# Small vector steps of a first attention layer moved from VectorE to ScalarE and GpSimd, in a three-layer attention program

## The chip, the cores and the metric

The program runs on one core of one Trainium2 chip, as one launch. The metric is the device time of that core in microseconds. Before the change the median of three runs is 1432.54 us (1431.04 to 1433.38).

## What is computed

Sixteen sequences of 256 tokens by 128 channels pass through a gated depthwise convolution, an attention whose softmax is taken apart in chunks of 64 keys, a layer norm, and then two layers of windowed attention with a gated MLP. The change touches only the first part. Cut to what matters, in float32:

```python
context = x.mean(axis=1)
gate = sigmoid(context @ w_kgen.T + b_kgen).mean(axis=1)        # one number a sequence, of 3 sigmoids
y = (depthwise_conv3(x) + b_conv) * gate                        # 3 taps over the tokens
q, k, v = y @ w_q.T, y @ w_k.T, y @ w_v.T                       # 16 query heads, 4 key heads, 64 wide
w = softmax(q @ k.T / 8) inside each chunk c of 64 keys         # 4 chunks
sum_w = w.sum(-1)                                               # the share of each chunk
out = sum_c(sum_w[c] * (w[c] @ v[c])) / (sum_c(sum_w[c]) + 1e-9)
x = layernorm(x + out @ w_o.T)
```

The kernel applies one factor to the exponentials of each head and chunk: with s their sum, the share is s * (1/s), the total adds the four shares and 1e-9, and the factor is (1/s) * share / total.

## The kernel before

Every engine has its own instruction stream, written out by hand, and streams meet only at semaphores. The first attention ("stage A") goes through the sequences two to a turn, in 8 turns. A sequence has two tiles of 128 queries, and a tile has four steps, g = 0 to 3, one for each key head with its four query heads. So a sequence takes 8 steps, and each engine's `a_body` walks through the same steps. At step s:

- TensorE (PE) transposes the scaled exponentials of step s-7 (L1291, into `wT`'s banks), computes the scores of step s (L1304), at some steps fills a bank for the sequence after this one (transposes of x, gate logits, at tile 1 the projections q, k and v from `hT`: L1264, L1266, L1268), multiplies the transposed weights of step s-7 by v (L1330), and at g = 3 does the output projection (L1341). The scores of step s need the subtraction of step s-2, since two pairs of banks hold them.
- VectorE (DVE) takes the maxima `mx` of the scores (L1030) and subtracts them (L1036, into `probs`), and adds up the exponentials of step s-2 (L1004, `sums`). At g = 1 this sum stands ahead of the step's maxima and is the last of a tile, so the factors `coef` follow at once (L989 to L996, seven short instructions, each waiting for the one before). The convolution `conv` of the next sequence stands at tile 0, g = 2 (L947 to L953), its gate and `hT` at tile 1, g = 0 (L959 to L967), the residual sum `y` and its statistics `mv` at g = 3 (L1053 to L1059), the end of the layer norm `xo` at g = 2 (L1065).
- ScalarE (ACT) copies `wT` out of its banks (L783), then projections (L757, L762, L767), then takes the exponentials of step s-1 (L796) and copies `oT` (L802).
- GpSimd (POOL) multiplies `probs` of step s-5 by `coef` (L625), so that a tile's four products begin at g = 1, and computes the layer norm's 1/sqrt (L636, L639) at g = 0. In the first turn it also splits the layers' weights into two parts (L613, L615), in steps 0 to 5, after a wait for all weights and four table products (L607).
- SyncE (SP) issues the DMAs; none of its code changes.

After the last turn a "drain" finishes the late steps and already begins with the layers that follow.

## Time and profile before

| what | us |
|---|---|
| median of three runs | 1432.54 |
| the profiled execution, its own time | 1430.35 |
| its span on the core | 1428.5 |
| stage A, up to the last maxima and subtractions | about 655 |
| the layers behind it | the rest, about 770 |

The profile shows each instruction with its start and duration, from one execution. In rows that group instructions ("lines"), the columns are: line, engine, operation, output<-inputs, shapes, count, then busy us and mean ns of one, then the idle us of the engine just before them and who ended it. A timeline row has start us, duration us, engine, line, operation, names, shapes, count, and in brackets the idle time before it. The duration of a run of instructions (x2) is from its first start to its last end. On PE each matrix product of float32 shows as two records. Neighbours overlap by some 0.08 us: differences of starts add up exactly, durations do not.

### The profile page before, as it was taken

The numbers are of one execution on the slowest core, as the hardware profiler recorded it, in microseconds if no ns is written. First come the engines' busy times: TensorE is split into PE (matmuls) and PEld (weight loads), VectorE is DVE, ScalarE is ACT, GpSimd is POOL, SyncE is SP. The second block draws the span as 40 slices with busy tenths as digits, with TensorE's granted clock in tenths as the row PEclk, the third lists the DMA queues.
The fourth block names the chain that finished last, engine by engine and source line by source line (L and its number), as shares of the span: only waits on it lengthen the run. The fifth ranks groups of instructions, "written<-read, shape, count | busy, mean of one in ns | idle before, by whom it ended". The sixth has DMA issues, their size and how long they took to land.

```text
span 1428.5 us, 36014 instructions
## 1 busy us (share of the span) xinstructions
PE 1258.4 (88%) x12288; PEld 984.8 (69%) x12288; DVE 1262.2 (88%) x2418; ACT 943.0 (66%) x1708; POOL 905.3 (63%) x787
## 2 busy tenths in 40 slices
PE   5889989998889898997789889898988999999985
PEld 3667767777667676775567777677776777777764
DVE  4999999999999999997688888888888899988974
ACT  3566666566666566564478777777877778787772
POOL 0733443344433443346798888888888899999972
PEclk8899999999999999999899999999999999999999
DMA  5000000000000000000111111121111211212111
GB/s 167 1 10 13 12 5 10 11 11 11 9 11 11 11 2 11 8 8 12 36 43 45 41 41 40 39 49 35 44 41 45 55 45 46 49 42 55 43 32 33
DMA packets 87051, 44.14 MB, mean 31 GB/s; under 512 B 43908, under 2 KB 80176, under 8 KB 86960
## 3 DMA queue, kind: packets, MB, share of 16 engines
q1 hardware_dynamic: 86960, 42.95, 12.0%
q8 instruction: 54, 0.88, 0.3%
q14 instruction: 37, 0.30, 0.1%
HBM read 19.86 MB, written 6.29 MB: 18 GB/s over the span
## 4 chain that ended last, share of the span: by engine, by line
DVE 45%; issue 19%; POOL 17%; PE 16%; DVEq 1%; ACT 1%; POOLq 0%; DMA 0%; SPq 0%; ACTq 0%
DVE sums L1004 9%; DVE probs L1036 7%; POOL rnorm L660 7%; DVE mx L1030 5%; POOL kT L668 4%; PE bank L1389 3%; POOL kT L649 3%; DVE xo L1065 2%; DVE hc L1102 2%; DVE qT L1084 2%; PE bank L1376 2%; PE bank L1473 2%; PE bank L1445 2%; DVE f_sum L1184 2%; DVE conv L947 1%
## 5 line engine op out<-in xcount | busy, mean ns | idle before, releaser
L625 POOL TENSOR_TENSOR probs<-probs,coef 128x1024 f32<-128x1024 f32 x128 | 239.5, 1901 | 201.0 <-DVE coef L996 201.0
L796 ACT ACTIVATE probs<-probs 128x1024 f32<-128x1024 f32 x128 | 134.8, 1053 | 98.8 <-DVE probs L1036 98.2
L649 POOL TENSOR_TENSOR kT<-qT 128x512 f32<-128x512 f32 x128 | 162.7, 1272 | 53.8 <-DVE qT L1084 53.6
L660 POOL TENSOR_TENSOR rnorm<-norm,halves 128x16 f32<-128x16 f32 x64 | 188.9, 2952 | 6.1 <-POOL norm L657 1.5
L1291 PE MATMUL bank<-ident,probs 128*128 128x128 f32 x1024 | 144.0, 286 | 49.2 <-POOL probs L625 49.2
L783 ACT ACTIVATE wT<-bank 128x512 f32<-128x512 f32 x256 | 138.6, 596 | 63.8 <-PE bank L1291 62.8
L1030 DVE TENSOR_REDUCE mx<-bank 128x8 f32<-128x512 f32 x256 | 164.0, 682 | 14.3 <-PE bank L1304 12.9
L1036 DVE TENSOR_TENSOR probs<-bank,mx 128x512 f32<-128x512 f32 x256 | 163.7, 682 | 0.0
L1291 PEld LDWEIGHTS bank<-ident,probs 128*128 128x128 f32 x1024 | 116.2, 145 | 68.3 <-POOL probs L625 57.4
L1304 PE MATMUL bank<-kT,qT 64*128 64x256 f32 x1024 | 157.2, 429 | 5.4 <-DVE probs L1036 5.4
L1004 DVE TENSOR_REDUCE sums<-probs 128x16 f32<-128x1024 f32 x128 | 153.4, 1211 | 0.0
L1330 PE MATMUL bank<-wT,v 128*64 128x128 f32 x2048 | 145.5, 286 | 8.6 <-DVE gate L942 4.7
L1202 DVE TENSOR_REDUCE fmx<-bank 128x4 f32<-128x512 f32 x128 | 82.5, 686 | 77.9 <-PE bank L1445 77.9
L1330 PEld LDWEIGHTS bank<-wT,v 128*64 128x64 f32 x2048 | 114.2, 141 | 47.3 <-issue 24.7
L668 POOL TENSOR_TENSOR kT<-kT,rnorm 128x512 f32<-128x512 f32 x128 | 131.1, 1045 | 4.3 <-POOL rnorm L660 0.7
L1304 PEld LDWEIGHTS bank<-kT,qT 64*128 64x128 f32 x1024 | 94.9, 200 | 37.1 <-issue 23.6
L1389 PE MATMUL bank<-hT,w 128*128 128x256 f32 (+1 forms) x384 | 97.5, 390 | 25.0 <-DVE mid L1167 23.2
L1376 PE MATMUL bank<-ident,kT 128*128 128x128 f32 x512 | 82.6, 285 | 38.6 <-POOL kT L668 37.3
L636 POOL TENSOR_TENSOR rstd<-mv,eps 128x1 f32<-128x1 f32 x32 | 6.2, 192 | 156.5 <-DVE mv L1059 156.5
L1376 PEld LDWEIGHTS bank<-ident,kT 128*128 128x128 f32 x512 | 57.0, 142 | 69.9 <-POOL kT L668 37.2
L721 POOL TENSOR_TENSOR probs<-probs,f_rsum 128x640 f32<-128x640 f32 x64 | 80.4, 1256 | 37.4 <-DVE f_rsum L1188 37.4
L1371 PE MATMUL bank<-wqkv_high,fhT_high 128*128 128x512 f32 x192 | 93.8, 489 | 3.9 <-DVE fhT_low L1152 1.0
(120 smaller groups left out, 3097.8 us busy)
## 6 DMA issues: line engine op xcount, KB each, us to landing
probs<-f_v SPq DMA_DIRECT2D x96, 128.0 KB, 2.3
res<-stage_x SPq DMA_DIRECT2D x48, 128.0 KB, 3.8
xn<-in_x SPq DMA_DIRECT2D x16, 128.0 KB, 2.2
xr<-in_x SPq DMA_DIRECT2D x16, 128.0 KB, 2.1
stage_x<-xo SPq DMA_DIRECT2D x32, 64.0 KB, 1.6
hn<-stage_x SPq DMA_DIRECT2D x32, 64.0 KB
mn<-mid SPq DMA_DIRECT2D x64, 32.0 KB
stage_x<-yo SPq DMA_DIRECT2D x16, 128.0 KB, 2.1
```

What stands on the lines that cost most here:

```text
L625: nc.gpsimd.tensor_tensor(out=e[:, :, :, :], in0=e[:, :, :, :], in1=coef[r][:, 2, A_REP * ng:A_REP * (ng + 1), :].unsqueeze(3).broadcast_t ...
L649: nc.gpsimd.tensor_tensor(out=qk[m][:, :, :], in0=on_self[m % 2][:, :, :], in1=on_partner[m % 2][:, :, :], op=ALU.add).then_inc(added, 1)
L660: nc.gpsimd.tensor_tensor(out=rnorm[:, at], in0=norm2[:, 1, at], in1=halves[:, 0:2 * F_HEADS], op=ALU.pow).then_inc(rnorm_set, 1)
L668: nc.gpsimd.tensor_tensor(out=qk[m][:, :, :], in0=qk[m][:, :, :], in1=rnorm[:, F_HEADS * m:F_HEADS * (m + 1)].unsqueeze(2).broadcast_to([P ...
L1004: nc.vector.tensor_reduce(sums[at % 2][:, A_REP * gg:A_REP * (gg + 1), :], E[(s - SUM_LAG) % E_RING][:, :, :, :], AX.X, ALU.add).then_inc( ...
L1030: ins = nc.vector.tensor_reduce(m[:, 2 * k:2 * k + 2, :], both[k][:, :].rearrange("p (h c k) -> p h c k", h=2, c=CHUNKS), AX.X, ALU.max)
L1036: ins = nc.vector.tensor_tensor(e[:, 2 * k:2 * k + 2, :, :], both[k][:, :].rearrange("p (h c k) -> p h c k", h=2, c=CHUNKS), m[:, 2 * k:2 ...
L1291: ins = nc.tensor.transpose(banks[4 + hp][:, P * (2 * kb + hh):P * (2 * kb + hh + 1)], e[:, 2 * hh + hp, 2 * kb:2 * kb + 2, :], ident[:, :])
L1304: ins = nc.tensor.matmul(banks[2 * (s % 2) + h % 2][:, SEQ * (h // 2):SEQ * (h // 2 + 1)], qT[p][lo:lo + A_HD, 2 * g + h // 2, P * tile:P ...
L1330: ins = nc.tensor.matmul(bank[A_HD * hh:A_HD * (hh + 1), P * hp:P * (hp + 1)], v[ap][:, kb, A_HD * og:A_HD * (og + 1)], wT[hp][:, kb, hh, ...
L1376: ins = nc.tensor.transpose(bank[:, P * block_of:P * (block_of + 1)], flat[:, P * block_of:P * (block_of + 1)], ident[:, :])
L1389: return nc.tensor.matmul(bank[0:rows, col:col + SEQ], w1[layer][:, at:at + rows], hT2[par][:, :], start=True, stop=True)
```

## The change

On VectorE only the two reciprocals of the factors, the reciprocal and the sum of the gate, and `y` with its statistics stay. The rest moves:

- The three taps of the convolution become three scaled copies on ScalarE (`taps`, tile 0, g = 1), added up by GpSimd (`convolution`, ahead of the product at tile 0, g = 2). The product with the gate (`gated_input`) and the end of the layer norm (`xo`) become scaled copies at the end of ScalarE's steps at tile 1, g = 0 and at g = 2. For `xo` GpSimd prepares a shift, the mean times -1 times 1/sqrt.
- GpSimd makes the shares, their total and the factors, ahead of a tile's first product (`shares`, `factors`), and the gate's denominators (`gate_denominator`, with the 1/3 of the mean in it).
- On VectorE the second reciprocal of the factors (`total_inverted`) stands between the maxima and the subtraction of g = 1, and the gate (`gated`) moves from ahead of the maxima at tile 1, g = 0 to behind the subtraction.
- On GpSimd the wait for the weights and the table products stand behind the first sequence's gate and convolution.

The diff, without the lines that define tiles, semaphores and constants, and without the bodies of the VectorE functions that go (they stand in the kernel above):

```diff
             pool.wait_ge(consts_set, N_CONSTS)
...
+            def shares(j, r):
+                c, tt, k = coef[r], total[r], SHARE_STEPS * j
+                pool.wait_ge(inverse_set, j + 1)
+                nc.gpsimd.tensor_tensor(out=c[:, 1, :, :], in0=sums[r][:, :, :], in1=c[:, 0, :, :], op=ALU.mult).then_inc(share_step, 1)
+                pool.wait_ge(share_step, k + 1)
+                nc.gpsimd.tensor_tensor(out=c[:, 2, :, 0:2], in0=c[:, 1, :, 0:2], in1=c[:, 1, :, 2:4], op=ALU.add).then_inc(share_step, 1)
+                pool.wait_ge(share_step, k + 2)
+                nc.gpsimd.tensor_tensor(out=tt[:, 0, :], in0=c[:, 2, :, 0], in1=c[:, 2, :, 1], op=ALU.add).then_inc(share_step, 1)
+                pool.wait_ge(share_step, k + 3)
+                nc.gpsimd.tensor_tensor(out=tt[:, 1, :], in0=tt[:, 0, :], in1=tiny[:, :], op=ALU.add).then_inc(share_step, 1)
+            def factors(j, r):
+                c, tt = coef[r], total[r]
+                pool.wait_ge(total_set, j + 1)
+                nc.gpsimd.tensor_tensor(out=c[:, 1, :, :], in0=c[:, 1, :, :],
+                                        in1=tt[:, 2, :].unsqueeze(2).broadcast_to([P, A_HEADS, CHUNKS]), op=ALU.mult).then_inc(coef_set, 1)
+                pool.wait_ge(coef_set, 2 * j + 1)
+                nc.gpsimd.tensor_tensor(out=c[:, 2, :, :], in0=c[:, 0, :, :], in1=c[:, 1, :, :], op=ALU.mult).then_inc(coef_set, 1)
+            def gate_denominator(b):
+                pool.wait_ge(gate_exp, b + 1)
+                nc.gpsimd.tensor_tensor(out=gate[:, 2, :], in0=gate[:, 1, :], in1=one3[:, 0, :], op=ALU.add).then_inc(gate_plus, 1)
+                pool.wait_ge(gate_plus, 2 * b + 1)
+                nc.gpsimd.tensor_tensor(out=gate[:, 2, :], in0=gate[:, 2, :], in1=one3[:, 1, :], op=ALU.mult).then_inc(gate_plus, 1)
+            def convolution(b):
+                pool.wait_ge(taps_set, b + 1)
+                nc.gpsimd.tensor_tensor(out=conv[:, 1, :], in0=conv[:, 0, :], in1=conv[:, 1, :], op=ALU.add).then_inc(conv_set, 1)
+                pool.wait_ge(conv_set, 2 * b + 1)
+                nc.gpsimd.tensor_tensor(out=conv[:, 2, :], in0=conv[:, 1, :], in1=conv[:, 2, :], op=ALU.add).then_inc(conv_set, 1)
...
                 for s, slot, p, tile, g in steps(i, turn, beside):
+                    if tile == 0 and g == 2 and prepares(turn, p):
+                        convolution(PAIR * i + p + 1)
+                    if tile == 1 and g == 0 and prepares(turn, p):
+                        gate_denominator(PAIR * i + p + 1)
                     if exists(turn, s, NORM_LAG):
...
                         r = at % 2
-                        wait(pool, coef_step, COEF_STEPS * (A_SLOTS * i + at + 1))
+                        if ng == 0:
+                            shares(A_SLOTS * i + at, r)
+                            factors(A_SLOTS * i + at, r)
+                        wait(pool, coef_set, 2 * (A_SLOTS * i + at + 1))
                         e = E[(s - NORM_LAG) % E_RING]
...
-            stage_a(pool, a_body)
+                        nc.gpsimd.tensor_tensor(out=rstd[r][:, 2:3], in0=mv[r][:, 0:1], in1=minus[:, 0:1], op=ALU.mult).then_inc(shift_set, 1)
+                        pool.wait_ge(rstd_set, j + 1)
+                        pool.wait_ge(shift_set, 2 * j + 1)
+                        nc.gpsimd.tensor_tensor(out=rstd[r][:, 3:4], in0=rstd[r][:, 2:3], in1=rstd[r][:, 1:2], op=ALU.mult).then_inc(shift_set, 1)
+            def a_pre():
+                gate_denominator(0)
+                convolution(0)
+                pool.wait_ge(weights_in, 16 * N_WEIGHTS)
+                for l in range(LAYERS):
+                    for tile in range(TILES):
+                        nc.gpsimd.tensor_tensor(out=table[l][:, tile, :, :], in0=rotary[:, tile, :, :], in1=qk_scale[l][:, :, :],
+                                                op=ALU.mult).then_inc(tables_set, 1)
+            stage_a(pool, a_body, a_pre)
...
+            def taps(b):
+                act.wait_ge(read["xT"], b + 1)
+                nc.scalar.activation(conv[:, 0, :], xT[:, 1:SEQ + 1], ACT.Identity, bias=bconv[:, 0:1], scale=wconv[:, 1:2])
+                nc.scalar.activation(conv[:, 1, :], xT[:, 0:SEQ], ACT.Copy, scale=wconv[:, 0:1])
+                nc.scalar.activation(conv[:, 2, :], xT[:, 2:SEQ + 2], ACT.Copy, scale=wconv[:, 2:3]).then_inc(taps_set, 1)
+            def gated_input(b):
+                act.wait_ge(conv_set, 2 * b + 2)
+                act.wait_ge(gate_step, GATE_STEPS * (b + 1))
+                wait(act, made["v"], b)
+                nc.scalar.activation(hT[:, :], conv[:, 2, :], ACT.Copy, scale=gate_sum[:, 0:1]).then_inc(hT_set, 1)
...
                 act.wait_ge(consts_set, N_CONSTS)
+                act.wait_ge(gate_weights_in, 16 * N_GATE_WEIGHTS)
                 x_transposed(0, 0, "pre", 0)
+                taps(0)
                 gate_exponential(0)
+                gated_input(0)
                 for kind, local in A_BANKS.pre[2:]:
...
                             x_transposed(i, p + 1, turn, PAIR * i + p + 1)
+                        if g == 1:
+                            taps(PAIR * i + p + 1)
                         if g == 3:
...
                                              banks[6 + A_BANKS.bank("o", s - PV_LAG, "middle")][:, 0:2 * P], ACT.Copy).then_inc(read["o"], 1)
+                    if prepares(turn, p) and tile == 1 and g == 0:
+                        gated_input(PAIR * i + p + 1)
+                    if g == LN_LAG % A_KV and exists(turn, s, LN_LAG):
+                        at = (s - LN_LAG) // A_KV
+                        j, r = A_SLOTS * i + at, at % 2
+                        act.wait_ge(shift_set, 2 * j + 2)
+                        wait(act, xo_out[r], 16 * (2 * i + at // 2))
+                        nc.scalar.activation(xo[r][:, :], y[r][:, :], ACT.Identity, bias=rstd[r][:, 3:4], scale=rstd[r][:, 1:2]).then_inc(xo_set, 1)
...
-            def convolution(b):
...
-                dve.wait_ge(gate_exp, b + 1)
-                nc.vector.tensor_scalar_add(gate[:, 2, :], gate[:, 1, :], 1.0).then_inc(gate_step, 1)
+                dve.wait_ge(gate_plus, 2 * b + 2)
+                nc.vector.reciprocal(gate[:, 3, :], gate[:, 2, :]).then_inc(gate_step, 1)
                 dve.wait_ge(gate_step, GATE_STEPS * b + 1)
-                nc.vector.reciprocal(gate[:, 3, :], gate[:, 2, :]).then_inc(gate_step, 1)
-                dve.wait_ge(gate_step, GATE_STEPS * b + 2)
+                wait(dve, hT_set, b)
                 nc.vector.tensor_reduce(gate_sum[:, :], gate[:, 3, :], AX.X, ALU.add).then_inc(gate_step, 1)
-                dve.wait_ge(gate_step, GATE_STEPS * b + 3)
-                dve.wait_ge(conv_step, 3 * b + 3)
-                wait(dve, made["v"], b)
-                nc.vector.tensor_scalar(hT[:, :], conv[:, 2, :], gate_sum[:, 0:1], 1.0 / KS,
-                                        ALU.mult, ALU.mult).then_inc(hT_set, 1)
...
                 gate_logit(0, 0, "pre")
-                convolution(0)
                 gated(0)
...
-            def factors(j, r):
...
+            def inverted(j, r):
                 dve.wait_ge(sum_done, A_KV * (j + 1))
-                wait(dve, normed, A_KV * (j - 1))
-                link(nc.vector.reciprocal(c[:, 0, :, :], sums[r][:, :, :]), 1)
-                link(nc.vector.tensor_tensor(c[:, 1, :, :], sums[r][:, :, :], c[:, 0, :, :], ALU.mult), 2)
-                link(nc.vector.tensor_reduce(tt[:, 0, :], c[:, 1, :, :], AX.X, ALU.add), 3)
-                link(nc.vector.tensor_scalar_add(tt[:, 1, :], tt[:, 0, :], 1e-9), 4)
-                link(nc.vector.reciprocal(tt[:, 2, :], tt[:, 1, :]), 5)
-                link(nc.vector.tensor_tensor(c[:, 1, :, :], c[:, 1, :, :],
-                                             tt[:, 2, :].unsqueeze(2).broadcast_to([P, A_HEADS, CHUNKS]), ALU.mult), 6)
-                link(nc.vector.tensor_tensor(c[:, 2, :, :], c[:, 0, :, :], c[:, 1, :, :], ALU.mult), 7)
+                nc.vector.reciprocal(coef[r][:, 0, :, :], sums[r][:, :, :]).then_inc(inverse_set, 1)
+            def total_inverted(i, turn, s):
+                if exists(turn, s, SUM_LAG):
+                    at = (s - SUM_LAG) // A_KV
+                    j, r = A_SLOTS * i + at, at % 2
+                    dve.wait_ge(share_step, SHARE_STEPS * (j + 1))
+                    nc.vector.reciprocal(total[r][:, 2, :], total[r][:, 1, :]).then_inc(total_set, 1)
...
                     dve.wait_ge(exp_done, n + 1)
+                    if gg == 0:
+                        wait(dve, coef_set, 2 * (A_SLOTS * i + at - 1))
                     nc.vector.tensor_reduce(sums[at % 2][:, A_REP * gg:A_REP * (gg + 1), :], E[(s - SUM_LAG) % E_RING][:, :, :, :],
...
                     if gg == A_KV - 1:
-                        factors(A_SLOTS * i + at, at % 2)
+                        inverted(A_SLOTS * i + at, at % 2)
...
                         gate_weights(PAIR * i + p + 1)
-                    if tile == 1 and g == 0 and prepares(turn, p):
-                        gated(PAIR * i + p + 1)
                     if g == 1:
...
                             ins.then_inc(max_set, 1)
+                        if g == 1:
+                            total_inverted(i, turn, s)
                         wait(dve, wT_made, 2 * (n - E_RING) + 2)
...
                         ins.then_inc(sub_done, 1)
+                    elif g == 1:
+                        total_inverted(i, turn, s)
                     if tile == 0 and g == 2 and prepares(turn, p):
                         gate_logit(PAIR * i + p + 1, p + 1, turn)
+                    if tile == 1 and g == 0 and prepares(turn, p):
+                        gated(PAIR * i + p + 1)
                     if g != 1:
                         summed(i, turn, s)
-                    if prepares(turn, p):
-                        b = PAIR * i + p + 1
-                        if tile == 0 and g == 2:
-                            convolution(b)
                     if g == OUT_LAG % A_KV and exists(turn, s, OUT_LAG):
...
                         dve.wait_ge(made["out"], j + 1)
+                        wait(dve, xo_set, j - 1)
                         dve.wait_ge(xr_in[(at // TILES) % 2], 16 * (i + at // TILES // PAIR + 1))
...
                         nc.vector.bn_aggr(mv[r][:, :], stat[r][:, :]).then_inc(y_step, 1)
-                    if g == LN_LAG % A_KV and exists(turn, s, LN_LAG):
-                        at = (s - LN_LAG) // A_KV
-                        j, r = A_SLOTS * i + at, at % 2
-                        dve.wait_ge(rstd_set, j + 1)
-                        wait(dve, xo_out[r], 16 * (2 * i + at // 2))
-                        nc.vector.tensor_scalar(xo[r][:, :], y[r][:, :], mv[r][:, 0:1], rstd[r][:, 1:2],
-                                                ALU.subtract, ALU.mult).then_inc(xo_set, 1)
```

How the order of instructions changes, at three places. A row is a line of the program, an operation, and its names and output shape. First VectorE, from the gated input at tile 1, g = 0, to the maxima of g = 1. Before:

```order
L967 TENSOR_SCALAR hT<-conv,gate_sum 128x256
L1030 TENSOR_REDUCE mx<-bank 128x8 x2
L1036 TENSOR_TENSOR probs<-bank,mx 128x512 x2
L1004 TENSOR_REDUCE sums<-probs 128x16 x2
L989 RECIPROCAL coef<-sums 128x64
L990 TENSOR_TENSOR coef<-sums,coef 128x64
L991 TENSOR_REDUCE total<-coef 128x16
L992 TENSOR_SCALAR total<-total 128x16
L993 RECIPROCAL total<-total 128x16
L994 TENSOR_TENSOR coef<-coef,total 128x64
L996 TENSOR_TENSOR coef<-coef 128x64
L1030 TENSOR_REDUCE mx<-bank 128x8 x2
```

The same stretch after the change:

```order
L1087 TENSOR_REDUCE mx<-bank 128x8 x2
L1095 TENSOR_TENSOR probs<-bank,mx 128x512 x2
L1030 RECIPROCAL gate<-gate 128x3
L1033 TENSOR_REDUCE gate_sum<-gate 128x1
L1063 TENSOR_REDUCE sums<-probs 128x16 x2
L1045 RECIPROCAL coef<-sums 128x64
L1087 TENSOR_REDUCE mx<-bank 128x8 x2
L1053 RECIPROCAL total<-total 128x16
L1095 TENSOR_TENSOR probs<-bank,mx 128x512 x2
```

The five steps between the two sums and the maxima have become one, the second reciprocal has moved in behind the maxima, and the gate's two steps stand behind the subtraction.

GpSimd's stream in one sequence, from one tile's factors to the end of its products. After the change (before it, only the products, L625, stand here):

```order
L622 TENSOR_TENSOR coef<-sums,coef 128x64
L624 TENSOR_TENSOR coef<-coef 128x16x2
L626 TENSOR_TENSOR total<-coef 128x16
L628 TENSOR_TENSOR total<-total,tiny 128x16
L634 TENSOR_TENSOR coef<-coef,total 128x64
L637 TENSOR_TENSOR coef<-coef 128x64
L667 TENSOR_TENSOR probs<-probs,coef 128x1024
L649 TENSOR_TENSOR conv<-conv 128x256
L651 TENSOR_TENSOR conv<-conv 128x256
L667 TENSOR_TENSOR probs<-probs,coef 128x1024 x2
L642 TENSOR_TENSOR gate<-gate,one 128x3
L644 TENSOR_TENSOR gate<-gate,one 128x3
```

Six small instructions now stand ahead of a tile's first product, two of the convolution between the first and the second, and two of the gate between the third and the fourth.

GpSimd in the first turn, at the weights' splits. Before:

```order
L613 CAST wqkv_high<-wqkv 128x512
L615 TENSOR_TENSOR wqkv_low<-wqkv,wqkv_high 128x512
L613 CAST wqkv_high<-wqkv 128x512
L615 TENSOR_TENSOR wqkv_low<-wqkv,wqkv_high 128x512
L625 TENSOR_TENSOR probs<-probs,coef 128x1024
L613 CAST wqkv_high<-wqkv 128x512
L615 TENSOR_TENSOR wqkv_low<-wqkv,wqkv_high 128x512
L625 TENSOR_TENSOR probs<-probs,coef 128x1024 x7
```

After, from the end of the second split (of six) to the first factors:

```order
L615 TENSOR_TENSOR wqkv_low<-wqkv,wqkv_high 128x512
L649 TENSOR_TENSOR conv<-conv 128x256
L651 TENSOR_TENSOR conv<-conv 128x256
L613 CAST wqkv_high<-wqkv 128x512
L615 TENSOR_TENSOR wqkv_low<-wqkv,wqkv_high 128x512
L613 CAST wqkv_high<-wqkv 128x512
L615 TENSOR_TENSOR wqkv_low<-wqkv,wqkv_high 128x512
L642 TENSOR_TENSOR gate<-gate,one 128x3
L644 TENSOR_TENSOR gate<-gate,one 128x3
L613 CAST wqkv_high<-wqkv 128x512
L615 TENSOR_TENSOR wqkv_low<-wqkv,wqkv_high 128x512
L622 TENSOR_TENSOR coef<-sums,coef 128x64
```

The second sequence's convolution stands behind two splits and its gate behind four.

## Rows read from the trace of the kernel before

**Rows 1.** The profile's page, its first part.

```profile
PE 1258.4 (88%) x12288; PEld 984.8 (69%) x12288; DVE 1262.2 (88%) x2418; ACT 943.0 (66%) x1708; POOL 905.3 (63%) x787
```

**Rows 2.** Busy us (instructions) of PE, PEld, DVE, ACT, POOL; then granted clock.

```profile
148.50:590.60 442.10, 397.62 (x3474) 311.62 (x3474) 428.26 (x782) 271.93 (x485) 180.65 (x133) 0.97 0.03 10
```

**Rows 3.** PE, groups by line, from 148.5 to 590.6 us.

```profile
L1291 PE MATMUL bank<-ident,probs 128*128 128x128 f32 x704 | 98.3, 284 | 29.9 <-POOL probs L625 29.9
L1264 PE MATMUL bank<-hT,wq 128*128 128x256 f32 x176 | 46.5, 397 | 9.8 <-DVE hT L967 9.8
...
L1247 PE MATMUL bank<-ident,xn 128*128 128x128 f32 x22 | 4.8, 300 | 0.0
L1254 PE MATMUL bank<-wk_ctx,ones 128*128 128x3 f32 x22 | 4.2, 263 | 0.0
```

**Rows 4.** VectorE, timeline of one tile's last sum, factors and next maxima.

```profile
301.19 1.21 DVE L1004 TENSOR_REDUCE sums<-probs 128x16 f32<-128x1024 f32 x1
302.43 0.55 DVE L989 RECIPROCAL coef<-sums 128x64 f32<-128x64 f32 x1
...
304.43 1.28 DVE L1030 TENSOR_REDUCE mx<-bank 128x8 f32<-128x512 f32 x2
305.63 1.28 DVE L1036 TENSOR_TENSOR probs<-bank,mx 128x512 f32<-128x512 f32 x2
```

**Rows 5.** VectorE, groups by line, from 148.5 to 590.6 us.

```profile
L1065 DVE TENSOR_SCALAR xo<-y,mv,rstd 128x128 f32<-128x128 f32 x22 | 23.8, 1081 | 0.0
L947 DVE TENSOR_SCALAR conv<-xT,wconv,bconv 128x256 f32<-128x256 f32 x11 | 20.0, 1815 | 0.0
...
L993 DVE RECIPROCAL total<-total 128x16 f32<-128x16 f32 x22 | 5.6, 253 | 0.8
L953 DVE SCALAR_TENSOR_TENSOR conv<-xT,wconv,conv 128x256 f32<-128x256 f32 x11 | 5.3, 485 | 0.4
...
L994 DVE TENSOR_TENSOR coef<-coef,total 128x64 f32<-128x64 f32 x22 | 5.0, 225 | 0.8
```

**Rows 6.** PE, timeline: a wait and what follows it; then two steps without waits.

```profile
306.55 1.09 PE L1291 MATMUL bank<-ident,probs 128*128 128x128 f32 x8 [1.85 <-POOL probs L625]
307.57 2.03 PE L1304 MATMUL bank<-kT,qT 64*128 64x256 f32 x8
...
617.44 1.13 PE L1304 MATMUL bank<-kT,qT 64*128 64x256 f32 x8
...
620.55 1.13 PE L1304 MATMUL bank<-kT,qT 64*128 64x256 f32 x8
```

**Rows 7.** GpSimd, groups by line: two from 148.5 us on, two from 640 us on.

```profile
L625 POOL TENSOR_TENSOR probs<-probs,coef 128x1024 f32<-128x1024 f32 x89 | 166.5, 1901 | 144.3 <-DVE coef L996 144.3
...
L636 POOL TENSOR_TENSOR rstd<-mv,eps 128x1 f32<-128x1 f32 x22 | 4.2, 190 | 115.1 <-DVE mv L1059 115.1
...
L649 POOL TENSOR_TENSOR kT<-qT 128x512 f32<-128x512 f32 x128 | 162.7, 1272 | 53.8 <-DVE qT L1084 53.6
...
L657 POOL TENSOR_SCALAR norm<-norm 128x16 f32<-128x16 f32 x64 | 16.1, 252 | 0.1
```

**Rows 8.** ScalarE, groups by line, from 148.5 to 590.6 us.

```profile
L802 ACT ACTIVATE oT<-bank 128x256 f32<-128x256 f32 x88 | 33.0, 375 | 7.1 <-PE bank L1330 6.4
```

**Rows 9.** Timelines of the first turn: GpSimd's tables; VectorE's gate; its maxima of step 8.

```profile
33.64 2.78 POOL L607 TENSOR_TENSOR table<-rotary,qk_scale 128x256 f32<-128x256 f32 x4 [31.72 <-DMA qk_scale<-in_k_scale]
...
36.35 0.16 DVE L959 TENSOR_SCALAR gate<-gate 128x3 f32<-128x3 f32 x1
...
57.01 1.29 DVE L1030 TENSOR_REDUCE mx<-bank 128x8 f32<-128x512 f32 x2 [1.42 <-PE bank L1304]
```

**Rows 10.** VectorE, timeline: two maxima one tile apart in the last sequence; the drain's end.

```profile
625.62 1.28 DVE L1030 TENSOR_REDUCE mx<-bank 128x8 f32<-128x512 f32 x2
...
644.38 1.28 DVE L1030 TENSOR_REDUCE mx<-bank 128x8 f32<-128x512 f32 x2
...
687.23 3.48 DVE L1065 TENSOR_SCALAR xo<-y,mv,rstd 128x128 f32<-128x128 f32 x1 [0.92 <-POOL rstd L639]
```

41 lines of the change are left out of this document (14 added, 27 removed).

## The prediction

> **What bounds the kernel now.** I read the page first, for the engines' shares: PE and VectorE both stand at 88% of the span [rows 1], which decides nothing, since stage A and the layers have different limits. So I cut out a stretch of the steady state: from 148.50 to 590.60 us the gate logits of eleven sequences pass, so a sequence takes 442.1 / 11 = 40.19 us. In it VectorE is busy for 428.26 us, 97%, PE for 397.62 (36.15 a sequence), GpSimd for 180.65 and ScalarE for 271.93 [rows 2]. The groups of PE then show that its idle time of 44.5 us is waiting for others: 29.9 for GpSimd's first product of a tile, which itself waits for `coef` from VectorE, and 9.8 for `hT`, also from VectorE [rows 3]. VectorE's own groups show next to no waits [rows 5]. VectorE sets the pace of stage A, and PE is 4 us a sequence behind it as the next limit.
>
> **What leaves VectorE.** In the eleven sequences `xo` costs 23.8 us and the first step of the convolution 20.0, the two others 5.3 each with 0.4 of dependency idle [rows 5]. The five factor steps that go are between 3.8 and 5.0 busy us each, 23.4 together, with about 4 us of idle between them (0.8 each, as in the row of L994). `hT` and the gate's first step make 5.4, with 0.9 idle. The sum is 43.8 + 10.6 + 0.8 + 27.4 + 6.3 = 89 us, or 8.1 us a sequence. That leaves 40.2 - 8.1 = 32.1 us of VectorE a sequence. Most of `xo` and of the convolution is no arithmetic: 1081 and 1815 ns on the mean, as they stand beside GpSimd's products. If only VectorE counted, 14 sequences would give back 113 us. But PE needs 36.15 us a sequence as its busy time stands, so I take PE as the next limit, and ask what it will wait for.
>
> **What PE will wait for at a tile's first product.** The chain from the scores of g = 0 to PE's transposes at g = 3 is now split over three engines. VectorE: maxima and subtraction 1.2 each (304.43 to 305.63 for one), sum of g = 0 1.12, with the 0.13 of `wk_ctx`, the last sum 1.24 (301.19 to 302.43), reciprocal 0.55: 5.44 us [rows 4]. Then GpSimd. For its small steps the trace has 190 ns for one element a partition, 252 for 16 (one input) and 1272 for 512 [rows 7]; a line through the first and the last gives 0.19 + 0.0021 a element, so 0.3 for 64, 0.25 for 32, 0.2 for 16. With 0.07 to 0.08 from one step to the next that depends on it, as between L989 and L990, the four steps of the shares are 0.07 + 0.30 + 0.08 + 0.25 + 0.08 + 0.2 + 0.08 + 0.2 = 1.3 us. Beside them VectorE does the maxima of g = 1, 1.2 us, so it waits 0.1 and this reciprocal, 0.25, comes at 1.35. Two more steps of 64, 0.75 with their gaps, and the product, 1.9 [rows 7], end 4.3 us after the first reciprocal. The whole is 0.1 + 5.44 + 4.3 = 9.85 us after the scores. PE in that time does the rest of step 0, steps 1 and 2: three steps of 3.11 (617.44 to 620.55), less the transposes and scores of step 0, 1.02 and 1.07 [rows 6], plus 0.44 for x and 0.38 for the gate logits [rows 3]: 8.1 us. So at tile 0 PE waits about 1.8 us. At tile 1 four fills of about 1 us (46.5 us for 44 of them [rows 3]) stand in place of the 0.8: 11.1 against 9.85 + 0.4 for the gate: no wait, 0.9 of slack. Bounds of the six small GpSimd steps, of 1.5 us in all: 190 ns each from below would take 0.3 off; VectorE's 225 ns for 64 [rows 5] times GpSimd's 1.27 to VectorE's 0.64 at 512 (half of 1.28, rows 4) gives 0.42 each, or about 1 us more with the short rows of four elements; I take the line, as it passes through this engine's own rows.
>
> The Trainium skill ("GPSIMD Engine Reference", section 4.1) puts elementwise work on VectorE and calls GpSimd about 2x slower for two inputs, which speaks against these six steps. By it 64 elements would be 0.45 us instead of 0.3, the tile's wait some 0.7 us longer and the whole change worth 10 us less. The row of 190 ns for one element says that the fixed part is no larger than VectorE's, so I don't take it for the small ones.
>
> **The gated input.** `hT` was ahead of the maxima of tile 1, g = 0; now the gate stands behind the subtraction, and ScalarE makes `hT` at the end of its step. From the scores: 0.1 + 2.4 + 0.4 + 0.07 + 0.35 + 0.1 = 3.4 us, against 3.1 of PE (products of step 4, transposes and scores of step 5). PE waits 0.3. ScalarE is held there until 0.35 us before, and its copies `wT` of the next step come late, but end before PE has done its two fills, 1.9 us.
>
> **What costs nothing.** ScalarE gains three taps, `hT` and two `xo` a sequence, at most 375 ns each like `oT` [rows 8], 2.2 us on 24.7; the exponentials that the taps push back by 0.9 are wanted by VectorE a step later. GpSimd gains 2 x 1.5 for the factors, 2 x 0.7 for the convolution, 0.5 for the gate and 2 x 0.4 for the shift, on 16.4: it is busy 22 of 38 us. The convolution's steps delay the second product by 1.4 us, PE wants that 5 us after the first. If ScalarE's cover went, each late `wT` would cost PE its length, 0.6 us.
>
> **The slow clock.** After the wait of 1.85 us PE's scores take 2.03 us instead of 1.13 [rows 6]; the granted clock of the stretch is 0.97 of 2.4 GHz [rows 2]. PE's 36.15 a sequence holds that share; with waits of the same length once a sequence I leave it in.
>
> **The sum.** A sequence takes 36.15 + 1.8 + 0.3 = 38.2 us, 2.0 less than now. That holds for the 14 sequences from step 8 to the last that prepares another: -28 us.
>
> First turn: GpSimd is free for work only when the weights are there, 33.64, and the tables done, 36.4 [rows 9]. Then come two splits of 1.95, the second sequence's convolution 1.4, two splits, and the gate 0.5: 46.1. VectorE wanted the gate at 36.35 and now stands until 46.1, ahead of two sums and the first reciprocal, which ends at 49.4. Shares to first product: 53.6, where it was 48.1. PE then has the transposes, scores, two fills, products and the next transposes and scores, 7.2 us: the maxima of step 8 come at about 61, where they were at 57.01 [rows 9]. +4 us, between +2 (if the splits overlap what VectorE had lost there anyway) and +7.
>
> Last sequence: no fills, so PE's step stretch is 7.25 and the wait 2.6; a tile is 14.3 (four steps of 3.11, and 1.9 for the output projection's sixteen records at the pace of eight transposes in 1.02) + 2.6 + about 1.5 for slow clock = 18.4 against 18.76 [rows 10]: -0.6 for two, between -4 and +2. Drain: `xo` on VectorE stands 3.48 us behind GpSimd's clears, and the first scores of the layers wait for what is behind it [rows 10]; on ScalarE it is short, -2; GpSimd's longer chain gives back 1: -1. The layers don't change.
>
> 1430.35 + 4 - 28 - 0.6 - 1 = 1404.8 for an execution like the profiled one, which lies 2.2 us under the median of 1432.54. On the median: 1407, and I say 1406.
>
> **Rivals.**
> - *The handover is hidden, and PE runs without waits.* For it: VectorE would have 4 us of slack a sequence, and the wait of tile 0 is a difference of two sums of 8 and 10 us. Against: it would take 1.8 us less on a chain whose long parts are rows. 36.15 a sequence: 14 x -4.0 + 2.4 = 1377 to 1383, say 1380. 15%.
> - *GpSimd's small steps take 0.4 to 0.5 us, or the slow clock comes with each wait.* One us more at tile 0 (tile 1 keeps its slack), or 0.9 more of slow products a sequence: 14 us back, 1420. For it: the wait of 1.85 did bring the slow clock; against: in this stretch only about every second did. 20%.
> - *Slower: GpSimd's handover becomes the limit.* Place: the six steps ahead of a tile's first product. Each us added costs 1 us at tile 0 and, beyond 0.9, 1 us at tile 1; with 2.0 us of gain a sequence the change loses from 1.5 us added on, that is from 0.5 us a small step. At 0.75 us each, 3 us added, a sequence takes 38.2 + 3 + 2.1 = 43.3, and the program 1432 + 14 x 3.1 + 2 = 1478. For it: the steps read rows of 2 or 4 elements or one in four, which no row of GpSimd here shows. Against: 252 ns for 16 elements. 10%.
> - *VectorE's two new waits* (shares ahead of the subtraction, the gate's denominators) *eat the slack*, so that stage A keeps its pace: 1430 to 1435. It needs 6 us a sequence of waiting. 5%.
>
> **How the numbers follow.** The forecast has 50%; its own range, from the bounds above (0.3 less and 1 more on the chain of tile 0, +2 to +7 in the first turn, -4 to +2 at the end), is 1396 to 1419. With the two neighbours the range that should hold 8 in 10 is 1384 to 1427. About 0.2%, 3 us, is what a measurement of this kernel can tell from no change. Faster by more than that: 50 + 15 + 18 = 83%; within it 5% (the last rival and the upper edge of the second); slower 12%.
>
> **What would show it.** In a stretch of eleven sequences: 38.2 us each; VectorE near 85% busy, PE near 95%; PE's waits for GpSimd at tile 0 near 1.8 us and none at tile 1; its wait for `hT` at 0.3; GpSimd's six steps 0.2 to 0.3 us each; VectorE's wait ahead of the second reciprocal 0.1. In the first turn a stand of VectorE from 37 to 46 us. It would be wrong if small GpSimd steps are above 0.5 us, if `wT` waits on ScalarE appear in PE's list in microseconds, or if PE's busy time moves by more than 0.9 us a sequence from 36.15.

## The result, and the profile after

| what | median us (runs) | ratio to before, 95% interval |
|---|---|---|
| before, beside it | 1432.21 (4) | |
| after | 1419.45 (1417.34 to 1420.7, 4) | 0.9909 (0.9892 to 0.9927) |

The change makes the program 12.8 us faster. The forecast was 1406, 26 us faster: the sign was right, and a little less than half of the gain came. 1419.45 lies just outside the forecast's own range (1396 to 1419), inside the wide one. One run of the kernel of experiment 10 below, of 2333 us, was disturbed and is in no interval.

The first part of the page of the kernel after answers to [rows 1], and the windows answer to [rows 2]. The first window holds eleven sequences, from one gate logit to another, the second the rest of stage A, up to the layers' first scores.

```profile
PE 1252.5 (88%) x12288; PEld 978.7 (69%) x12288; DVE 1146.5 (81%) x2146; ACT 976.5 (69%) x1804; POOL 996.2 (70%) x1111
```

```profile
153.19:583.77 430.58, 396.04 (x3479) 308.78 (x3477) 352.08 (x595) 293.66 (x550) 243.18 (x352) 0.98 0.04 10
...
583.80:685.30 101.50, 86.28 (x765) 68.23 (x763) 65.91 (x112) 55.34 (x101) 66.27 (x86) 0.92 0.04 11
```

A sequence now takes 430.58 / 11 = 39.14 us, where it took 40.19. VectorE went from 97% to 352.08 / 430.58 = 82% busy (85% were forecast), so it left the path as forecast. PE is busy 36.00 us a sequence, also as forecast (36.15), but that is 92% of the sequence and not the 95% of the forecast. The other 3.14 us are waits, and the groups of PE, which answer to [rows 3], name them:

```profile
L1382 PE MATMUL bank<-wT,v 128*64 128x128 f32 x1408 | 100.4, 287 | 8.6 <-ACT qT L826 8.6
L1343 PE MATMUL bank<-ident,probs 128*128 128x128 f32 x707 | 95.4, 278 | 21.7 <-POOL probs L667 21.7
L1316 PE MATMUL bank<-hT,wq 128*128 128x256 f32 x176 | 46.5, 397 | 4.2 <-ACT hT L814 4.2
```

21.7 / 11 = 1.97 us is the wait for the first product at tile 0 (none at tile 1), 0.38 the wait for `hT`, and 0.78 is a wait for ScalarE that the forecast did not have. 36.00 + 1.97 + 0.78 + 0.38 = 39.13.

The handover, in the timelines of VectorE, GpSimd and PE after (start us, us, engine, ...), beside [rows 4, 6]:

```profile
304.46 0.55 DVE L1045 RECIPROCAL coef<-sums 128x64 f32<-128x64 f32 x1
...
306.36 0.25 DVE L1053 RECIPROCAL total<-total 128x16 f32<-128x16 f32 x1 [0.21 <-POOL total L628]
...
305.09 0.32 POOL L622 TENSOR_TENSOR coef<-sums,coef 128x64 f32<-128x64 f32 x1 [5.13 <-DVE coef L1045]
305.49 0.24 POOL L624 TENSOR_TENSOR coef<-coef 128x32 f32<-128x32 f32 x1
305.81 0.22 POOL L626 TENSOR_TENSOR total<-coef 128x16 f32<-128x16 f32 x1
306.11 0.22 POOL L628 TENSOR_TENSOR total<-total,tiny 128x16 f32<-128x16 f32 x1
306.69 0.30 POOL L634 TENSOR_TENSOR coef<-coef,total 128x64 f32<-128x64 f32 x1 [0.37 <-DVE total L1053]
307.07 0.32 POOL L637 TENSOR_TENSOR coef<-coef 128x64 f32<-128x64 f32 x1
307.46 1.90 POOL L667 TENSOR_TENSOR probs<-probs,coef 128x1024 f32<-128x1024 f32 x1
...
309.42 1.09 PE L1343 MATMUL bank<-ident,probs 128*128 128x128 f32 x8 [1.98 <-POOL probs L667]
```

The six small steps take 0.22 to 0.32 us. From the reciprocal's end to the product's, 305.0 to 309.36, are 4.35 us; 4.3 were forecast.

Where the time went, in the two profiled executions: VectorE reads the third gate logit at 73.25 instead of 68.69 us (+4.6). From it to the sixteenth are 510.5 instead of 521.9 us (-11.4, thirteen sequences). From there to the layers' first scores are 101.6 instead of 103.4 (-1.8), and the layers are 1.0 shorter: -9.6 in the span (1428.5 to 1418.9). The profiled execution of before was its fastest and that of after its slowest, so this sum is 3 us short of the difference of the medians.

### The profile page after: what moved, and what is told of

Read it like the earlier page. It is cut to its first block, busy times and chain, and to the rows that moved or that the text cites. A ratio compares the mean times of both kernels' runs of the same rounds, so it can differ in the third digit from the quotient of the medians.

```text
span 1418.9 us, 36244 instructions
## 1 busy us (share of the span) xinstructions
PE 1252.5 (88%) x12288; PEld 978.7 (69%) x12288; DVE 1146.5 (81%) x2146; ACT 976.5 (69%) x1804; POOL 996.2 (70%) x1111
## 4 chain that ended last, share of the span: by engine, by line
POOL 33%; issue 25%; PE 21%; DVE 16%; ACT 2%; SPq 2%; POOLq 1%; DVEq 0%; DMA 0%; ACTq 0%
POOL probs L667 9%; POOL rnorm L715 7%; POOL kT L723 4%; PE bank L1441 3%; POOL kT L704 3%; DVE hc L1154 2%; PE bank L1428 2%; PE bank L1525 2%; PE bank L1356 2%; PE bank L1497 2%; DVE qT L1136 2%; DVE f_sum L1236 2%; PE bank L1343 2%; PE bank L1393 2%; POOL probs L776 1%
## 5 line engine op out<-in xcount | busy, mean ns | idle before, releaser
L1343 PE MATMUL bank<-ident,probs 128*128 128x128 f32 x1024 | 139.9, 280 | 37.3 <-POOL probs L667 37.3
L1382 PE MATMUL bank<-wT,v 128*64 128x128 f32 x2048 | 147.5, 289 | 13.7 <-ACT qT L826 11.4
L1343 PEld LDWEIGHTS bank<-ident,probs 128*128 128x128 f32 x1024 | 112.9, 142 | 55.4 <-POOL probs L667 42.0
L622 POOL TENSOR_TENSOR coef<-sums,coef 128x64 f32<-128x64 f32 x32 | 10.3, 321 | 151.7 <-DVE coef L1045 151.7
```

The lines of the kernel that those rows point to most:

```text
L1343: ins = nc.tensor.transpose(banks[4 + hp][:, P * (2 * kb + hh):P * (2 * kb + hh + 1)], e[:, 2 * hh + hp, 2 * kb:2 * kb + 2, :], ident[:, :])
L1382: ins = nc.tensor.matmul(bank[A_HD * hh:A_HD * (hh + 1), P * hp:P * (hp + 1)], v[ap][:, kb, A_HD * og:A_HD * (og + 1)], wT[hp][:, kb, hh, ...
```

## Experiments

Each stands as its median of 4 to 7 runs and its ratio to runs of the kernel before on the same chip. Differences in us, where nothing else is said, are of medians. The kernel before had 1430.96 us beside experiments 1 to 4 and 1431.70 to 1431.90 beside the others, against 1432.21 beside after, so such a difference to after can be 1 us off.

**1. Only `xo` moved.** The kernel before, with `xo` on ScalarE at g = 2 and its shift on GpSimd:

```diff
+ nc.gpsimd.tensor_tensor(out=rstd[r][:, 2:3], in0=mv[r][:, 0:1], in1=minus[:, 0:1], op=ALU.mult)        # and the shift, on GpSimd
...
+ nc.scalar.activation(xo[r][:, :], y[r][:, :], ACT.Identity, bias=rstd[r][:, 3:4], scale=rstd[r][:, 1:2])  # behind oT at g = 2
...
- nc.vector.tensor_scalar(xo[r][:, :], y[r][:, :], mv[r][:, 0:1], rstd[r][:, 1:2], ALU.subtract, ALU.mult)
```

> The kernel before with one part of the change alone: the end of the layer norm (xo) on ScalarE, with GpSimd's shift; convolution, gate, factors stay on VectorE. Theory (PE's waits are the limit behind VectorE, and little has to leave VectorE to reach it): VectorE loses 23.8 us in 11 sequences, 2.2 of 40.2 us a sequence, and PE's 36.0 plus its waits fit under the 38.0 left. About 38.0 to 38.5 us a sequence, 14 x 1.7 to 2.2 us = 24 to 30 us less than before: 1403 to 1408, faster than the whole change (1419). Rival (each part gives a share of the whole gain as its share of the 8.1 us taken off VectorE): 2.2/8.1 of 13 us, 1429.

Measured: 1410.31 us, 0.9857 (0.9842 to 0.9872), a little above the 1403 to 1408 of the theory. One of the moves alone gives 21 us (against 1430.96 beside it), more than all of them. A sequence takes 430.26 / 11 = 39.11 us here, where the theory had 38.0 to 38.5, and the granted clock is 1.00 where it was 0.98 after. Window and groups of PE in the same eleven sequences:

```profile
147.26:577.52 430.26, 388.66 (x3476) 304.29 (x3476) 407.01 (x761) 276.21 (x507) 188.33 (x177) 1.00 0.03 10
```

```profile
L1337 PE MATMUL bank<-wT,v 128*64 128x128 f32 x1408 | 96.3, 279 | 10.0 <-DVE gate L955 8.6 <-ACT qT L764 0.9
L1298 PE MATMUL bank<-ident,probs 128*128 128x128 f32 x704 | 94.9, 278 | 20.2 <-POOL probs L628 20.2
L1271 PE MATMUL bank<-hT,wq 128*128 128x256 f32 x176 | 46.5, 397 | 11.3 <-DVE hT L980 11.3
```

VectorE is 95% busy and already has 10.8 us of waits for scores, so 2 us off it are enough: it and PE now bound each other, and what else is taken off VectorE can only shorten PE's waits.

The whole change does shorten them, from 430.26 - 388.66 = 41.6 us here to 430.58 - 396.04 = 34.5 us in the eleven sequences. But PE is busy 396.04 us instead of 388.66. Here the waits for products are two a sequence, of 0.6 to 0.7 and 1.1 to 1.2 us, with no slow clock behind them; after, one of 1.97 us stands in their place, often with the slow clock behind it (experiment 4 shows the rows). The two kernels' thirteen sequences differ by only 2.3 us (508.2 against 510.5). The rest of this kernel's lead lies outside them: its third gate logit comes 4.0 us earlier, as it leaves the first turn almost as it was, and from the last gate logit to the layers it takes 95.5 us instead of 101.6, with a granted clock of 0.98 instead of 0.92.

**2. The factors back on VectorE**, all else as after: `shares` and `factors` go from GpSimd, the seven-step function comes back behind the last sum.

```diff
...
- nc.vector.reciprocal(coef[r][:, 0, :, :], sums[r][:, :, :]).then_inc(inverse_set, 1)
...
+ factors(j, r)        # the seven steps L989 to L996 of before
```

> The changed kernel with one part undone: all seven factor steps on VectorE ahead of the maxima again; convolution, gate, xo stay moved. Theory (the handover to GpSimd and back sets PE's wait at tile 0): from the first reciprocal to GpSimd's first product 2.16 us instead of 3.0, PE's wait at tile 0 falls from 1.98 to about 1.1 us, VectorE has 34.4 us of work a sequence and still waits for PE. 14 x 0.85 = 12 us less than the changed kernel: about 1407. Rival (VectorE's load is what counts, any work given back to it costs): 1.15 us later maxima twice a sequence, +14 to +32 us: 1433 to 1450.

Measured: 1410.45 us, 0.9863 (0.9848 to 0.9879): 9 us better than after (7 by the ratios). PE's wait for the first product falls from 1.97 to 12.9 / 11 = 1.17 us, and its busy time from 36.00 to 388.77 / 11 = 35.34, with the clock at 1.00.

```profile
L1359 PE MATMUL bank<-wT,v 128*64 128x128 f32 x1408 | 96.3, 279 | 17.2 <-DVE gate L1000 8.6 <-ACT qT L802 8.6
L1320 PE MATMUL bank<-ident,probs 128*128 128x128 f32 x704 | 94.9, 278 | 12.9 <-POOL probs L643 12.9
```

The shorter chain is not the whole reason, though. VectorE now reads the gate logits late, and PE waits 8.6 / 11 = 0.78 us for their bank, which it did not after; the wait for `hT` grows from 0.38 to 0.63 us. All of PE's waits together went up, from 3.14 to 3.36 us a sequence. What fell is the time that it is busy: without one long wait, no group ran at the slow clock. So in this order of the kernel the split of the factor chain over two engines costs more than it gives, and the cost shows in the clock.

**3. TensorE's output projection ahead of the products at g = 3.** A test of my first reading of the 0.78 us, that PE waits there for `wT`. The table that gives the fills of banks 6 and 7 their order changes with it.

```diff
+ if g == OUT_LAG % A_KV and exists(turn, s, OUT_LAG):   # the output projection, moved up
      if late:                                            # the products of wT and v
```

> The changed kernel, with PE's output projection at g = 3 ahead of the products with v instead of behind them. Theory (PE's new wait of 0.79 us at tile 1, g = 3 is for wT copies that ScalarE makes late, behind kT, the exponentials, oT and xo, once a sequence): the 1.9 us of output projection cover it, 14 x 0.79 = 11 us less than the changed kernel: about 1408. Rival (ScalarE as a whole is behind, and the wait turns up at the next place that needs it): within 3 us of 1419.

Measured: 1426.19 us, 0.9967 (0.9956 to 0.9978). The theory falls, and 7 us more than after is outside the rival's 3 us too. The wait moved whole to the projection:

```profile
L1376 PE MATMUL bank<-wo,oT 128*128 128x128 f32 x352 | 49.3, 297 | 8.6 <-ACT qT L826 8.6
```

So it belongs to whatever comes first after the last fills at g = 3. The two banks 6 and 7 alternate, and the next user of the bank of the last q waits until ScalarE has read that q. ScalarE's timeline after, with the PE row that waits, shows why it reads late:

```profile
291.07 1.06 ACT L870 ACTIVATE probs<-probs 128x1024 f32<-128x1024 f32 x1
292.15 0.38 ACT L876 ACTIVATE oT<-bank 128x256 f32<-128x256 f32 x1
292.43 0.48 ACT L885 ACTIVATE xo<-y,rstd 128x128 f32<-128x128 f32 x1
292.81 1.07 ACT L855 ACTIVATE wT<-bank 128x512 f32<-128x512 f32 x2
293.77 0.60 ACT L826 ACTIVATE qT<-bank 128x512 f32<-128x512 f32 x1
...
294.50 1.09 PE L1382 MATMUL bank<-wT,v 128*64 128x128 f32 x16 [0.79 <-ACT qT L826]
```

PE filled the bank by 292.7; ScalarE comes to it at 293.77, behind the exponentials, `oT`, the new `xo` and two `wT`, on which PE would not have waited. Why this kernel is slower than after I followed only in part: eight of its thirteen sequences are slow ones, of 40.2 to 40.4 us, where after has seven of 39.9 to 40.0 (see the next experiment), and the others are 0.1 to 0.3 us longer too.

**4. The scores too ahead of the transposes at g = 3.** The transposes of g = 3 wait for the first product; the scores don't.

```diff
# on top of the edit of experiment 3; the two parts of the step stand in functions
- for part in (transposes, scores_of):
+ for part in ((scores_of, transposes) if g == OUT_LAG % A_KV else (transposes, scores_of)):
```

> As the run with the output projection first, and at g = 3 PE also does its scores ahead of its transposes. Theory (the wait of 1.98 us at tile 0 is the chain over VectorE and GpSimd, and PE has 1.07 us of scores that do not depend on it): the wait falls to 0.6 to 1.0 us, and with it the slow clock after it may go, 0 to 0.75 us a sequence. 14 x 1.0 to 1.7 us beyond the last run: 1385 to 1394. Rival (the scores of g = 3 wait themselves for the subtraction of g = 1, which is part of the same chain): no gain beyond the last run, 1408.

Measured: 1395.05 us, 0.9751 (0.9738 to 0.9765), 24 us under after and 31 under experiment 3, at the edge of the 1385 to 1394 of the theory. The wait of 1.97 became two short ones, as PE's timeline at tile 0 shows:

```profile
296.90 1.14 PE L1359 MATMUL bank<-kT,qT 64*128 64x256 f32 x8 [0.37 <-DVE probs L1095]
298.51 1.09 PE L1344 MATMUL bank<-ident,probs 128*128 128x128 f32 x8 [0.47 <-POOL probs L667]
```

The sequences show the rest of the gain. Between gate logits after there are two lengths, 38.4 to 38.5 and 39.9 to 40.0 us, seven of the thirteen long. In experiment 4 all thirteen lie between 37.55 and 37.76. A long one of after has the slow clock behind its wait:

```profile
190.94 1.09 PE L1343 MATMUL bank<-ident,probs 128*128 128x128 f32 x8 [1.97 <-POOL probs L667]
191.96 2.02 PE L1356 MATMUL bank<-kT,qT 64*128 64x256 f32 x8
193.91 1.83 PE L1382 MATMUL bank<-wT,v 128*64 128x128 f32 x16
```

From 192.0 to 195.6 us the granted clock is 0.53, and 1.00 in the group before and behind. In the thirteen sequences together experiment 4 is 20.9 us shorter than after (489.6 against 510.5): 13 x 1.13 = 15 us are the shorter waits, and seven long sequences less, at 1.4 us each, are 10; some 4 us are lost again, a part of it in a longer wait for `hT` (5.2 / 11 = 0.47 us). The 0.78 us for q's bank are still there.

**5. `xo` one step later** (g = 3, behind the copy of q).

```diff
- EXP_LAG, SUM_LAG, NORM_LAG, PV_LAG, OUT_LAG, LN_LAG = 1, 2, 5, 7, 11, 14
+ EXP_LAG, SUM_LAG, NORM_LAG, PV_LAG, OUT_LAG, LN_LAG = 1, 2, 5, 7, 11, 15
```

> The changed kernel with one number changed: the layer norm's lag is 15 steps instead of 14, so xo stands on ScalarE at g = 3 instead of g = 2. Theory (PE's wait of 0.79 us once a sequence is for a bank that ScalarE has to read, the last q, and ScalarE comes to it late behind kT, exponentials, oT, xo and wT; xo is 0.38 us of that): the wait falls to about 0.41 us; 14 x 0.38 = 5 us less than the changed kernel, 1414. Rival (that wait has nothing to do with ScalarE's moved work): within 2 us of 1419.

Measured: 1410.15 us (1405.88 to 1414.7), 0.9854 (0.9832 to 0.9876). PE's wait for q's bank falls by half:

```profile
L1382 PE MATMUL bank<-wT,v 128*64 128x128 f32 x1408 | 98.8, 284 | 4.5 <-ACT qT L826 4.5
```

4.5 / 11 = 0.41 us a sequence, 0.38 less, which is 5 us over thirteen: the theory's 5 us are there, and the kernel gained more. In the profiled executions two long sequences fewer (five instead of seven) give 3 us, and from the last gate logit to the layers are 97.7 us instead of 101.6, with a granted clock of 0.97 instead of 0.92. The five runs of this kernel lie 9 us apart, so its 9 us are less certain than the others' gains.

**6. The gate ahead of the maxima again**, as before the change.

```diff
+ if tile == 1 and g == 0 and prepares(turn, p):   # ahead of the maxima
+     gated(PAIR * i + p + 1)
- ...                                               # behind the subtraction
```

> The changed kernel with the gate's two steps on VectorE ahead of the maxima of tile 1, g = 0, where they were before the change. Theory: PE's wait for hT, 0.38 us a sequence, goes, since ScalarE has what it needs 2.7 us earlier: 14 x 0.38 = 5 us less, 1414. Rival (GpSimd's denominators come too late for that place, VectorE waits there and hands the wait on): 1419 or more.

Measured: 1406.21 us, 0.9818 (0.9804 to 0.9832). The wait for `hT` goes from 4.2 to 0.0 us in eleven sequences, 0.38 each; five of thirteen sequences are long. The place of the gate cost 13 us: 5 by its own wait, 3 by two long sequences more, and 4.5 between the last gate logit and the layers (101.6 against 97.1 us), where the granted clock is 0.97 here and 0.92 after.

**7. GpSimd's tables and splits of the first turn later** (the tables at step 8, the splits at steps 9 to 14).

```diff
- if turn == "first" and s < 3 * LAYERS:
-     split_weights(*divmod(s, 3))
+ if turn == "first" and s == 8:      # the wait for the weights and the four table products, out of a_pre
...
+ if turn == "first" and 8 < s <= 8 + 3 * LAYERS:
+     split_weights(*divmod(s - 9, 3))
```

> The changed kernel with GpSimd's table products at step 8 and its weight splits at steps 9 to 14 of the first turn, instead of ahead of step 0 and at steps 0 to 5. Theory (VectorE's stand of 7.7 us and PE's of 10.2 us in the first turn is for two small gate steps queued behind the wait for the weights, tables and four splits): the third gate logits come 4.6 us or more earlier than in the changed kernel, as in the kernel before or better; 5 to 9 us less: 1410 to 1414. Rival (what is early there is lost again when the splits stand beside the products): within 2 us of 1419.

Measured: 1409.88 us, 0.9851 (0.9838 to 0.9865). The third gate logit comes at 65.84 instead of 73.25 us and the sequences stay as they were, 39.15 us. The cost of the first turn was real. Timelines of GpSimd and VectorE after, beside [rows 9]:

```profile
33.44 2.78 POOL L694 TENSOR_TENSOR table<-rotary,qk_scale 128x256 f32<-128x256 f32 x4 [21.76 <-DMA qk_scale<-in_k_scale]
...
45.52 0.20 POOL L644 TENSOR_TENSOR gate<-gate,one 128x3 f32<-128x3 f32 x1
...
45.75 0.18 DVE L1030 RECIPROCAL gate<-gate 128x3 f32<-128x3 f32 x1 [7.70 <-POOL gate L644]
...
62.75 1.29 DVE L1087 TENSOR_REDUCE mx<-bank 128x8 f32<-128x512 f32 x2 [2.81 <-PE bank L1356]
```

**8. The edits of 4, 5, 6 and 7 together.**

> The changed kernel with all four edits: output projection ahead of the products and scores ahead of the transposes at g = 3 (1395 by itself), xo at g = 3, the gate ahead of the maxima, GpSimd's tables and splits later. Theory (the waits of PE add up one by one): 1395 - 5 - 6 - 5 to 9 = 1375 to 1380. Rival (the waits overlap, what one edit takes away another wait takes): 1388 or more.

Measured: 1379.04 us (1378.12 to 1380.34), 0.9633 (0.9619 to 0.9646), the fastest version of all and inside the 1375 to 1380 of the theory. The lengths of the waits add up, the measured gains don't: 24, 9, 13 and 10 us by themselves make 56, and together they are 40. Experiments 4, 5 and 6 each had a part of the same slow clock in their gain, and it can be saved only once. No sequence but the first is long, and in the next twelve PE is 426.42 of 441.40 us busy:

```profile
104.13:545.53 441.40, 426.42 (x3795) 331.25 (x3793) 380.82 (x649) 318.11 (x600) 265.09 (x384) 1.00 0.04 11
```

**9. The order of experiment 4 in the kernel before.** Is that order good by itself?

> The kernel before, with only TensorE's order changed at g = 3 (the output projection ahead of the products, the scores ahead of the transposes), the same edit that took 24 us off the changed kernel. My theory: before the change VectorE sets the pace (428 of 442 us busy in the steady state), so PE's waits are slack and reordering it gives nothing: 1430 us, between 1424 and 1434, a sequence of 40.1 us with VectorE 97% busy. Rival: PE's wait for the first product and the slow clock behind it were the cost already in the kernel before, and the order alone gives most of the 24 us: 1405 to 1412, a sequence near 38.5.

Measured: 1452.05 us, 1.0137 (1.0122 to 1.0152): slower, which neither side had expected. A sequence takes 40.6 to 43.5 us. PE's groups over the twelve sequences from 112.9 us on, and VectorE's timeline ahead of one long wait of PE:

```profile
L1307 PE MATMUL bank<-kT,qT 64*128 64x256 f32 x768 | 114.6, 419 | 19.0 <-DVE probs L1036 19.0
...
L1344 PE MATMUL bank<-wT,v 128*64 128x128 f32 x1536 | 109.2, 286 | 29.5 <-DVE y L1053 29.5
```

```profile
321.86 1.81 DVE L947 TENSOR_SCALAR conv<-xT,wconv,bconv 128x256 f32<-128x256 f32 x1
323.71 0.48 DVE L950 SCALAR_TENSOR_TENSOR conv<-xT,wconv,conv 128x256 f32<-128x256 f32 x1
...
324.63 0.34 DVE L1065 TENSOR_SCALAR xo<-y,mv,rstd 128x128 f32<-128x128 f32 x1
...
328.41 0.28 DVE L1053 TENSOR_TENSOR y<-bank,xr 128x128 f32<-128x128 f32 x1
...
328.82 1.10 PE L1344 MATMUL bank<-wT,v 128*64 128x128 f32 x16 [2.71 <-DVE y L1053]
```

Convolution and `xo` stand ahead of the maxima, subtraction and sum that `y` is behind, and the projection's bank is wanted sooner in this order. So the same order pays 24 us in a kernel whose VectorE has 18% of slack and costs 20 us in one whose VectorE has 3%.

**10. The factors back on VectorE, on top of experiment 8** (the edit of experiment 2).

> The kernel with all four edits (1379 us), with the factors made on VectorE again. My theory: taking them off VectorE pays nothing there either, since PE is 35.5 of 36.8 us a sequence busy and its wait for the first product is 0.43 of that; VectorE has 31.7 + 2.5 = 34.2 us of work a sequence, still under PE: 1376 us, between 1370 and 1382, PE's wait for GpSimd at 0 to 0.4. Rival: with 34.2 of 36.8 us VectorE has too little slack between its bursts, the exponentials or the scores' banks come late, and the kernel is slower: 1385 to 1395, with PE's waits for VectorE (0.42 a sequence) above 1.0.

Measured: 1397.51 us, 0.9764 (0.9749 to 0.9779), 18 us slower than experiment 8: the rival holds, at a time a little above its 1385 to 1395. A sequence takes 37.9 to 38.0 us instead of 36.8, and PE's groups show the wait, of 1.6 us once a sequence; VectorE's and PE's timelines show its cause:

```profile
L1337 PE MATMUL bank<-kT,qT 64*128 64x256 f32 x768 | 109.8, 405 | 19.0 <-DVE probs L1077 19.0
```

```profile
323.91 0.56 DVE L1030 RECIPROCAL coef<-sums 128x64 f32<-128x64 f32 x1
...
325.91 1.28 DVE L1071 TENSOR_REDUCE mx<-bank 128x8 f32<-128x512 f32 x2
327.11 1.27 DVE L1077 TENSOR_TENSOR probs<-bank,mx 128x512 f32<-128x512 f32 x2
...
328.44 1.13 PE L1337 MATMUL bank<-kT,qT 64*128 64x256 f32 x8 [1.64 <-DVE probs L1077]
```

From the reciprocal to the maxima are 2.0 us; in experiment 8 they are 0.5 (319.02 to 319.49). The factor chain on VectorE holds up the next subtraction, and with it the bank of the next scores. The same move of the factors costs 9 us where PE waits for the product (2), and gives 18 us where PE waits for the subtraction (8 against 10).

## Why the prediction was half right

- **What bounds it.** Right: VectorE left the path and PE with its waits took it, as the first window shows. PE's busy time, 36.00 for 36.15, is right too.
- **The handover at tile 0.** 1.97 us for 1.8, and none at tile 1. The line through GpSimd's own rows [rows 7] held: 0.32, 0.24 and 0.22 us for 64, 32 and 16 elements. By the 2x of the Trainium skill ("GPSIMD Engine Reference", section 4.1) the estimate for 64 would have been 0.45; the trace has 0.30 to 0.32, of which 0.19 is what one element takes.
- **`hT`.** 0.38 us for 0.3.
- **"What costs nothing": the step that failed.** The forecast said that ScalarE's new work "costs nothing", with `wT` as the only thing looked at. PE's 0.78 us a sequence were there, not at `wT` but at the bank of the last q. Over thirteen sequences it is 10 us of the 14 by which they missed the forecast (510.5 against 13 x 38.2 = 497). Experiment 3 showed that it is a bank's wait, experiment 5 that `xo` is half of it; what makes the other 0.41 us, which are there in experiment 8 too, stays open. `xo` on ScalarE does not make the wait by itself: in experiment 1 it is 0.9 us in eleven sequences together. PE has other waits there (for the gate logits' bank and 1.03 us for `hT`) and may simply come later; that was not tested. The sizes were not what failed. ScalarE's records of the moved operations are longer than the 375 ns that the forecast took from `oT` [rows 8]:

```profile
L885 ACT ACTIVATE xo<-y,rstd 128x128 f32<-128x128 f32 x22 | 10.6, 483 | 0.0
L805 ACT ACTIVATE conv<-xT,bconv,wconv 128x256 f32<-128x256 f32 x11 | 6.7, 607 | 0.0
L814 ACT ACTIVATE hT<-conv,gate_sum 128x256 f32<-128x256 f32 x11 | 5.6, 508 | 15.3 <-DVE gate_sum L1033 15.3
```

But neighbours overlap: in the timeline of after that experiment 3 shows, `xo` starts at 292.43 and the next one at 292.81, 0.38 us later, the 0.38 that experiment 5 took off the wait. All the new work made ScalarE 293.66 - 271.93 = 21.7 us busier in eleven sequences, 2.0 a sequence for 2.2 forecast.
- **The slow clock.** Its share was left in, and on the mean that was right for the steady state (36.00 for 36.15). What the forecast did not see is that a change in PE's waits can move this share: PE's busy time is 35.33 and 35.34 us in experiments 1 and 2, and experiments 5 and 6 removed 5 us of waits each and gave 9 and 13.
- **The end.** From the last gate logit to the layers -1.8 us where -3.6, with the fourteenth sequence's -2.0, were forecast. The granted clock there is 0.92, and 0.90 in the same stretch of before. How the miss divides between waits and clock stays open.
- **First turn.** +4.6 us for +4; VectorE's stand ended at 45.75, as forecast (46.1), and step 8's maxima came at 62.75 for 61. Experiment 7 gives it back.
- **The rivals.** The second, 1420, has the size by luck, as neither of its reasons came: the small steps took 0.22 to 0.32 us, and PE's busy time did not rise over 36.15. The slower one, GpSimd's handover as the limit, did not occur.

The miss in the thirteen sequences is 14 us: 10.1 for q's bank (13 x 0.78), 3.3 for the handover and `hT` (13 x 0.25), less 2.0 for PE's busy time (13 x 0.15), and the rest, some 2, mostly for the first two sequences, which are both long (39.98 and 39.96 us). The layers' -1.0 us I did not follow.

The forecast's own range was also narrower than the bounds that it names: 14 us for 1 us more at tile 0, 3 for the first turn and 2.6 for the end add up to 1425 or 1426 from 1406, not to 1419. The measured time lies inside that, but the bound that makes it so, slower GpSimd steps, is not what happened.
